# Sharing the expert outputs of a Perceiver block's mixture of experts among VectorE, ScalarE and GpSimd, and reordering the work around them

## The chip, the cores and the metric

The kernel runs on one core of a Trainium2 chip. The metric is the device time of one execution in microseconds; lower is better. The engines work side by side and are ordered by semaphores: TensorE (PE in the profile, its weight loads PEld), VectorE (DVE), ScalarE (ACT), GpSimd (POOL) and the sync engine (SP), which issues the DMAs. Each engine carries out its own instructions strictly in the order in which the program lists them.

## The reference

All numbers are float32. `x` holds 64 sequences of 32 rows of 256. Three sublayers follow one another, each added to `x`:

1. cross-attention to 257 context rows per sequence (4 heads, the 32 highest scores of each row kept), with a gain and shift from the attended context, a 32-step sequence convolution done by a real Fourier product, and a feed-forward part 256 -> 1024 -> 256;
2. self-attention over the 32 rows of each sequence (in the kernel called tile part c);
3. a mixture of 8 experts (tile part dd). For each row: `logits = x @ w_route.T` plus a product with normalized centroids; a softmax over the two highest logits gives `gate[8]`, zero elsewhere; then

```
out = x + sum_k gate[k] * (gelu(xn @ w1[k] + b1[k]) @ w2[k] + b2[k])      # k = 0..7, xn = layernorm(x)
```

## The kernel before

The 2048 rows are 16 tiles of 128 rows (4 sequences each). The kernel is a software pipeline that is written out by hand: 18 steps after a first one, and in step n four different tiles are at four stages: `a` (tile n: scores and the search for the 32 highest), `b` (tile n-1: attended context, gain and shift, Fourier convolution, first feed-forward product), `c` (tile n-2: end of the feed-forward part, self-attention) and `dd` (tile n-3: mixture of experts). Steps 3 to 15 hold all four; steps 16 to 18 run empty. There is one `step` function for each engine, and the order of the lines in it is the engine's order of work. `wait(engine, semaphore, value)` holds up the engine, and all that is listed behind it. The conditions are plain integers, since all steps are unrolled.

What the names around the change mean:

- `xl3` is the normalized input of the experts (L854 on VectorE, the first work of a step there; it is placed right behind L982 of the step before). PE transposes it at L1009 as the first thing after `down`, ahead of `scores(0)`. The two hidden products of the experts are `wide(0, D1, ...)` and `wide(1, D0, ...)`, 16 matmuls each (L1054), into the PSUM banks D1 and D0.
- `gelus(act2, 0, ...)` and `gelus(act2, 1, ...)` (L538) turn them into `act2` on ScalarE. In the step they stand behind the copy of `gateT` (L592, L593), which waits for PE's transpose of `gate` (L1135).
- `experts(range(...))` on PE multiplies `act2[k]` by `e_w2[k]` (L1071); experts 0, 1 go to D1, 2, 3 to D0, 4, 5 to D1, 6, 7 to D0. "Expert 8" is the product of `gateT` (8 rows) with `e_b2` (8 rows), the gated biases (L1069). A bank is overwritten after VectorE has read it.
- `gated(range(...))` on VectorE reads the banks: L842 and L844 start two sums `acc[0]` and `acc[1]`, L848 adds experts 2 to 7 to them in turn, L850 adds expert 8, and L982 adds the two sums into `out_sb`.
- `weights(t, q)` on GpSimd (L498, two instructions) makes `wsel[2q]`, `wsel[2q+1]` from VectorE's `rsum_row` (L833). PE's product `am` (L1101) of tile b needs all four. `norm(k, tile)` (L469 to L476) and `length(tile)` (L478 to L489) are chains of small GpSimd instructions that turn a variance into `rstd[k]` and `inorm`.
- `take(a, q)`, `top8`, `find8`, `take8` and `probs` on VectorE search for the 32 highest scores and make the attention weights; `probs(b, 1)` ends in L833.

GpSimd's order within a step is, shortened:

```
weights(b, 1); tm_tile (L503); xb_c (L507); norm(1, c); norm(2, c); norm(0, b); xt_b (L512); norm(3, c); length(c); weights(a, 0)
```

and VectorE's order at the end of one step and the start of the next:

```
top8(a,1,1); gated(6,8); top8(a,1,2); gated(8,9); L982   ||   L854 xl3; top8(b,1,3); probs(b,1) -> L833; L863; ...
```

Of the kernel before, what the change touches and what calls it, by code (L numbers as in the profile page):

```python
# [88 lines left out]
def build(nc, d, out):  # L89
    with ExitStack() as ctx:  # L90
# [6 lines left out]
        def sem(name):  # L97
            return ctx.enter_context(nc.semaphore(name))
# [27 lines left out]
        e_b2 = sb("e_b2", [NE, D])  # L126
# [18 lines left out]
        def over(buf, *shape):  # L145
# [7 lines left out]
            if len(shape) == 2:  # L153
# [55 lines left out]
        acc = [over("ang", D) for _ in range(2)]  # L209
        dots = sb("dots", [128, 2 * NE])  # L210
# [8 lines left out]
        gateT = sb("gateT", [NE, 128])  # L219
# [64 lines left out]
                 "xl3_v xT3_mm xT3_a lg_mm dots_a nbest_v ed_a gate_v gT_mm gT_a e1a_mm e1b_mm g2a_a g2b_a eo_mm acc_v fin_v").split()  # L284
# [3 lines left out]
        passed_v, passed_g = sem("passed_v"), sem("passed_g")  # L288
# [25 lines left out]
        def _(sp):  # L314
# [15 lines left out]
            for h in range(H):  # L330
# [9 lines left out]
            load(anyb[:, :], any_dram.rearrange("b o -> o b").broadcast_to([128, NB]), "ld_any")  # L340
            late_loads = [
# [9 lines left out]
                (e_b1[:, :], d["e_b1"], "ld_w"), (e_b2[:, :], d["e_b2"], "ld_w"),  # L351
# [44 lines left out]
        def _(pool):  # L396
# [26 lines left out]
            pool.wait_ge(s["fills"], 3)  # L423
            nc.gpsimd.memset(qk2[64:65, :, :, :], 1.0).then_inc(s["fills"], 1)
            nc.gpsimd.memset(zT2[64:65, :], 1.0).then_inc(s["fills"], 1)
            pool.wait_ge(s["fills"], 5)
# [64 lines left out]
            def step(a, b, c, dd):  # L491
                def weights(t, q):

                    wait_apart(pool, chains["tm"], t.count(1, 1), passed_g)
                    wait_apart(pool, s["rsum_v"], t.count(2, q + 1), passed_g)
                    wait_apart(pool, s["am_mm"], t.count(1, 0), passed_g)
                    for k in (2 * q, 2 * q + 1):
                        nc.gpsimd.tensor_scalar(wsel[:, k, :], sel[:, :], rsum_row[:, k:k + 1], tm_tile[:, k:k + 1], ALU.mult, ALU.mult).then_inc(s["wsel_g"], 1)  # L498
                if b:
                    weights(b, 1)  # L500
                if a:
                    wait_apart(pool, s["wsel_g"], a.count(4, 0), passed_g)
                    nc.gpsimd.tensor_copy(tm_tile[:, :], text_m[:, bass.ds(a.n * BT, BT)]).then_inc(chains["tm"], 1)  # L503
                if c:

                    wait_apart(pool, s["x1_v"], c.count(1, 0), passed_g)
                    nc.gpsimd.tensor_tensor(xb_c[:, :], x_all[:, c.n, :], bout[:, :], ALU.add).then_inc(s["xb_g"], 1)  # L507
                    norm(1, c)
                    norm(2, c)
                if b:  # L510
                    norm(0, b)
                    nc.gpsimd.tensor_tensor(xt_b[:, :], xt[:, :], b2[:, :], ALU.add).then_inc(s["xtb_g"], 1)  # L512
                if c:
                    norm(3, c)
                    length(c)
                if a:
                    weights(a, 0)

# [10 lines left out]
        def _(act):  # L529
# [31 lines left out]
            def step(a, b, c, dd, setup=None):  # L561
# [65 lines left out]
            act.wait_ge(s["fills"], 5)  # L627
# [29 lines left out]
        def _(dve):  # L657
# [128 lines left out]
            def step(a, b, c, dd):  # L786
# [48 lines left out]
                def gated(ks):  # L835

                    for k in ks:
                        bank = (D1, D0)[k // 2 % 2][:, k % 2 * D:k % 2 * D + D]
                        wait(dve, s["eo_mm"], dd.count(NE + 1, min(k // 2 * 2 + 2, NE + 1)))
                        if k == 0:  # L840
                            wait(dve, s["gate_v"], one(dd))
                            V.scalar_tensor_tensor(acc[0][:, :], bank, gate[:, 0:1], x2[dd.p][:, :], ALU.mult, ALU.add).then_inc(s["acc_v"], 1)  # L842
                        elif k == 1:
                            V.tensor_scalar(acc[1][:, :], bank, gate[:, 1:2], None, ALU.mult).then_inc(s["acc_v"], 1)  # L844
                        else:
                            wait(dve, s["acc_v"], dd.count(NE + 1, k - 1))
                            if k < NE:
                                V.scalar_tensor_tensor(acc[k % 2][:, :], bank, gate[:, k:k + 1], acc[k % 2][:, :], ALU.mult, ALU.add).then_inc(s["acc_v"], 1)  # L848
                            else:
                                V.tensor_tensor(acc[0][:, :], bank, acc[0][:, :], ALU.add).then_inc(s["acc_v"], 1)  # L850
# [105 lines left out]
                if dd:  # L956
                    gated(range(2, 4))
# [47 lines left out]
        def _(pe):  # L1005
# [26 lines left out]
            def step(a, b, c, dd, setup=None):  # L1032
# [25 lines left out]
                def experts(ks):  # L1058
                    for k in ks:
# [24 lines left out]
                if dd:  # L1084
                    wait(pe, s["xl3_v"], one(dd))
                    wait(pe, s["acc_v"], dd.count(NE + 1, 0))
# [16 lines left out]
                if dd:  # L1103
                    wide(0, D1, e_w1, xT3, None, range(2))
# [64 lines left out]
                if c:  # L1169
# [6 lines left out]
                    ins.then_inc(s["v_mm"], 1)  # L1176
                if c:
# [7 lines left out]
                if dd:  # L1185
                    experts(range(2, 4))
# [40 lines left out]
            pe.wait_ge(s["fills"], 5)  # L1227
# [132 lines left out]
```

## Time and profile before

| | |
|---|---|
| time, median of 3 runs | 695.81 us (691.54 to 697.91) |
| time of the profiled execution | 698.97 us |
| its span, first to last instruction | 697.1 us |
| mean granted TensorE clock in the span | 0.921 of full speed |
| busy time PE, PEld | 600.1 us (86%), 428.8 us (62%) |
| busy time DVE, ACT, POOL | 530.2 us (76%), 317.8 us (46%), 221.5 us (32%) |
| one full step | 34.38 us |

The profiled execution lies 1.9 us outside its span. The start-up and the first steps take up to 171 us, the 13 full steps run from there to about 616 us, and the rest is the emptying pipeline. Busy shares are averages over these three stretches. The length of a full step is the distance of equal instructions in the time line.

### The profile page before, as it was taken

How to read it: one execution, taken by the hardware profiler on the slowest of the kernel's cores; microseconds unless marked ns; L12 is line 12 of the kernel's file. 1: busy time of each engine (PE TensorE's matmuls, PEld its weight loads, DVE VectorE, ACT ScalarE, POOL GpSimd, SP SyncE). 2: the span in 40 equal slices, each digit the busy share in tenths (PEclk: the TensorE clock that was granted, in tenths of full speed). 3: DMA queues.
4: the chain of work that ended last, by engine and by line, in shares of the span. 5: the costliest groups of instructions: out<-in, count | busy, mean ns of one | idle time of the engine just before them, and what ended most of it. 6: DMA issues, size and time to landing. Idle time of an engine off the chain costs nothing.

```text
span 697.1 us, 12267 instructions
## 1 busy us (share of the span) xinstructions
PE 600.1 (86%) x4142; PEld 428.8 (62%) x4142; DVE 530.2 (76%) x1817; ACT 317.8 (46%) x793; POOL 221.5 (32%) x580
## 2 busy tenths in 40 slices
PE   0359367899999999999999999999999999988776
PEld 0135133647686868686868686868686858575655
DVE  5579956557797979788888888888888888875242
ACT  6432011414646464646454555555555555444422
POOL 2540301215151515152424242424242424252320
PEclk9968555869999999999999999999999999999876
DMA  5396032030302030302030203020302020000000
GB/s 163 81 263 174 9 139 72 0 97 1 97 9 98 9 98 9 97 9 97 9 97 9 98 9 97 9 97 9 98 12 94 17 89 9 1 9 1 8 9 8
DMA packets 18439, 40.33 MB, mean 58 GB/s; under 512 B 5093, under 2 KB 11190, under 8 KB 17864
## 3 DMA queue, kind: packets, MB, share of 16 engines
q1 hardware_dynamic: 18376, 39.55, 18.2%
q8 instruction: 33, 0.54, 0.3%
q14 instruction: 30, 0.25, 0.1%
HBM read 37.37 MB, written 2.16 MB: 57 GB/s over the span
## 4 chain that ended last, share of the span: by engine, by line
PE 72%; DVE 13%; ACT 9%; DMA 2%; issue 2%; POOL 1%; SPq 1%; ACTq 0%; DVEq 0%
PE D L1071 9%; PE D L1054 9%; PE BB L1054 8%; PE BB L1077 7%; PE S L1030 4%; ACT L538 3%; PE S L1046 3%; PE S L1047 3%; ACT ang L538 3%; PE BB L1131 2%; PE BB L1167 2%; PE PC L1173 2%; PE BB L1168 2%; PE BB L1132 2%; PE PC L1175 2%
## 5 line engine op out<-in xcount | busy, mean ns | idle before, releaser
L473 POOL TENSOR_SCALAR var_in<-mv 128x1 f32<-128x1 f32 x64 | 14.1, 221 | 321.6 <-DVE mv L938 164.5
L1071 PE MATMUL D<-expw,ang 128*128 128x256 f32 x256 | 74.3, 417 | 10.0 <-ACT ang L538 9.5
L821 DVE MATCH_REPLACE8 work<-top,work 128x257 f32<-128x257 f32 x192 | 77.4, 411 | 0.0
L1054 PE MATMUL D<-ang,e_w 128*128 128x128 f32 x512 | 72.0, 287 | 0.0
L815 DVE MAX8 top<-work 128x8 f32<-128x257 f32 x192 | 71.5, 414 | 0.0
L1054 PEld LDWEIGHTS D<-ang,e_w 128*128 128x128 f32 x512 | 64.0, 198 | 10.1 <-issue 10.1
L1054 PEld LDWEIGHTS BB<-ang,w 128*128 128x128 f32 x512 | 59.7, 192 | 7.7 <-issue 6.0
L1071 PEld LDWEIGHTS D<-expw,ang 128*128 128x128 f32 x256 | 46.3, 200 | 23.9 <-ACT ang L538 15.7
L1054 PE MATMUL BB<-ang,w 128*128 128x128 f32 x512 | 60.0, 275 | 0.0
L1077 PE MATMUL BB<-expw,ang 128*128 128x256 f32 x256 | 57.9, 379 | 0.0
L1046 PE MATMUL S<-ctx_t,qk 128*128 128x257 f32 x128 | 45.0, 436 | 11.7 <-DMA ctx_l<-in_ctx_l 5.0
L1077 PEld LDWEIGHTS BB<-expw,ang 128*128 128x128 f32 x256 | 47.4, 190 | 5.8
L498 POOL TENSOR_SCALAR wsel<-sel,rsum_row,tm_tile 128x32 f32<-128x32 f32 x64 | 25.8, 414 | 56.4 <-issue 31.4
L848 DVE SCALAR_TENSOR_TENSOR ang<-D,gate,ang 128x256 f32<-128x256 f32 x96 | 41.4, 474 | 2.0 <-PE D L1071 2.0
L1047 PE MATMUL S<-ctx_t,qk 65*128 65x257 f32 x128 | 42.9, 419 | 0.0
L1030 PE MATMUL S<-q_diag,wk_w 128*128 128x512 f32 x64 | 39.1, 704 | 3.6 <-ACT q_diag L551 3.6
L538 ACT ACTIVATE ang<-BB,b 128x128 f32<-128x128 f32 x128 | 36.6, 368 | 10.6 <-PE BB L1054 10.5
L538 ACT ACT_TABLE_LOAD x32 | 41.1, 1283 | 0.5
L569 ACT ACTIVATE expo<-S,nmax 128x257 f32<-128x257 f32 x64 | 27.0, 473 | 31.1 <-DVE work L801 30.8
L1046 PEld LDWEIGHTS S<-ctx_t,qk 128*128 128x128 f32 x128 | 23.3, 210 | 28.3 <-issue 26.9
L475 POOL TENSOR_TENSOR rstd<-var_in,mhalf 128x1 f32<-128x1 f32 x64 | 36.5, 571 | 5.3
L569 ACT ACT_TABLE_LOAD x28 | 35.9, 1283 | 0.5
(245 smaller groups left out, 1250.1 us busy)
## 6 DMA issues: line engine op xcount, KB each, us to landing
ctx_n<-in_ctx_n SPq DMA_DIRECT2D x16, 768.0 KB
ctx_t<-in_ctxT SPq DMA_DIRECT2D x16, 514.0 KB
ctx_t<-in_ctxT SPq DMA_DIRECT2D x16, 257.0 KB
x_all<-in_x SPq DMA_DIRECT2D x4, 512.0 KB, 5.5
out<-out_sb SPq DMA_DIRECT2D x16, 128.0 KB, 1.7
ctx_l<-in_ctx_l SPq DMA_DIRECT2D x64, 24.0 KB
w<-in_W SPq DMA_DIRECT2D x1, 1024.0 KB
e_w<-in_e_w SPq DMA_DIRECT2D x1, 1024.0 KB, 4.8
```

Source lines behind the costliest of these rows:

```text
L475: link(tt(rstd[k][:, 0:1], w, mhalf[:, 0:1], ALU.pow))
L538: ins = A(dst[:, k, :], bank[:, 128 * (k % 4):128 * (k % 4) + 128], ACT.Gelu, bias=bias[:, k:k + 1])
L569: A(expo[:, 2 * q + k, :], S[k][:, 0:G], ACT.Exp, bias=nmax[:, 2 * q + k:2 * q + k + 1], scale=SCALE).then_inc(s["exp_a"], 1)
L815: V.max(top[:, 2 * q + k, 8 * r8:8 * r8 + 8], work[:, 2 * q + k, :]).then_inc(chains["top"], 1)
L821: V.match_replace(work[:, 2 * q + k, :], top[:, 2 * q + k, 8 * r8:8 * r8 + 8], work[:, 2 * q + k, :], TAKEN).then_inc(chains["taken"], 1)
L848: V.scalar_tensor_tensor(acc[k % 2][:, :], bank, gate[:, k:k + 1], acc[k % 2][:, :], ALU.mult, ALU.add).then_inc(s["acc_v"], 1)
L1030: MM(S[half][:, :], wk_w[:, half, :], q_diag[:, :, :].rearrange("p h t -> p (h t)"), start=True, stop=True).then_inc(s["qk_mm"], 1)
L1046: MM(bank[:, 0:G], qk1[:, k, :, :].rearrange("p h t -> p (h t)"), ctx_t1[a.p][:, k, :], start=True, stop=False)
L1047: MM(bank[:, 0:G], qk2[:, k, :, :].rearrange("p h t -> p (h t)"), ctx_t2[a.p][:, k, :], start=False, stop=True).then_inc(s["sc_mm"], 1)
L1054: ins = MM(bank[:, 128 * m:128 * m + 128], w[:, k, at:at + 128], xs[:, 128 * k:128 * k + 128], start=k == 0, stop=k == 1)
L1071: MM(bank, act2[:, k, :], e_w2[:, k, :], start=True, stop=True).then_inc(s["eo_mm"], 1)
L1077: ins = MM(B1[:, 0:D], act1[:, k, :], w2[:, k, :], start=k == 0, stop=k == HID // 128 - 1)
```

## The change

1. PE: experts 2 and 3 are multiplied behind `v_mm` and ahead of the self-attention scores (`s_mm`), no longer behind them.
2. ScalarE: the first four gelus of the experts stand ahead of the copy of `gateT`.
3. PE: the bias product of "expert 8" uses 128 rows, zero-filled: `gateT` and `e_b2` grow from 8 to 128 partitions, with two more fills on GpSimd at the start.
4. VectorE keeps experts 0, 1, 4, 5 and 8, all summed in `acc[0]`. Experts 2, 3, 6 and 7 are scaled by `gate` and copied out of bank D0 by ScalarE into `e_out` (`outputs(0)`, `outputs(1)`). GpSimd sums the four into `acc[1]` with three additions behind `length(c)`; the first stands ahead of `weights(a, 0)` and two stand behind it. VectorE's last addition waits for them (`acc_g`).
5. Two semaphores that the unrolled kernel never uses are gone.

```
 # sync engine
+            sp.wait_ge(s["fills"], 5)                       # ahead of the late loads; e_b2 is loaded into e_b2[0:NE]
 # GpSimd, start
-            pool.wait_ge(s["fills"], 3)
+            nc.gpsimd.memset(gateT[:, :], 0.0).then_inc(s["fills"], 1)
+            nc.gpsimd.memset(e_b2[:, :], 0.0).then_inc(s["fills"], 1)
+            pool.wait_ge(s["fills"], 5)
 # GpSimd, step
                 if c:
                     norm(3, c)
                     length(c)
+                if dd:
+                    wait(pool, s["ge_a"], dd.count(2, 1))
+                    wait(pool, s["fin_v"], dd.count(1, 0))
+                    nc.gpsimd.tensor_tensor(acc[1][:, :], e_out[:, 0, :], e_out[:, 1, :], ALU.add).then_inc(s["acc_g"], 1)
                 if a:
                     weights(a, 0)
+                if dd:
+                    wait(pool, s["ge_a"], dd.count(2, 2))
+                    for k in range(2):
+                        wait(pool, s["acc_g"], dd.count(3, k + 1))
+                        nc.gpsimd.tensor_tensor(acc[1][:, :], acc[1][:, :], e_out[:, 2 + k, :], ALU.add).then_inc(s["acc_g"], 1)
 # ScalarE, step
+                def outputs(half):
+                    wait(act, s["eo_mm"], dd.count(NE + 1, 4 * half + 4))
+                    wait(act, s["gate_v"], one(dd))
+                    wait(act, s["acc_g"], dd.count(3, 2 * half - 2))
+                    for k in range(2):
+                        ins = A(e_out[:, 2 * half + k, :], D0[:, k * D:k * D + D], ACT.Copy, scale=gate[:, 4 * half + 2 + k:4 * half + 3 + k])
+                    ins.then_inc(s["ge_a"], 1)
...
                 if dd:
+                    gelus(act2, 0, D1, e_b1, "e1a_mm", "g2a_a", dd)
                     wait(act, s["gT_mm"], one(dd))
-                    copy(gateT[:, :], PA[0:NE, 0:128], "gT_a")
-                    gelus(act2, 0, D1, e_b1, "e1a_mm", "g2a_a", dd)
+                    copy(gateT[0:NE, :], PA[0:NE, 0:128], "gT_a")
                     gelus(act2, 1, D0, e_b1, "e1b_mm", "g2b_a", dd)
...
                 if following:
                     transposed(following)
+                if dd:
+                    outputs(0)
                 if c:
                     ... (r_c copy)
                 if following:
                     query(following)
+                if dd:
+                    outputs(1)
 # VectorE, step: gated() goes over (0, 1, 4, 5, NE), always acc[0], each waits for the one before
-                if dd:
-                    gated(range(2, 4))
...
-                if dd:
-                    gated(range(6, 8))
                 if a:
                     top8(a, 1, 2)
                 if dd:
                     gated(range(8, NE + 1))
-                    wait(dve, s["acc_v"], dd.count(NE + 1, NE + 1))
+                    wait(dve, s["acc_v"], dd.count(5, 5))
+                    wait(dve, s["acc_g"], dd.count(3, 3))
                     wait(dve, st_out[dd.p], dd.half(16, 0))
                     V.tensor_tensor(out_sb[dd.p][:, :], acc[0][:, :], acc[1][:, :], ALU.add).then_inc(s["fin_v"], 1)
 # PE, step
-                        elif k >= 4 and k % 2 == 0:
-                            wait(pe, s["acc_v"], dd.count(NE + 1, k - 2))
+                        elif k == 6:
+                            wait(pe, s["ge_a"], dd.count(2, 1))
+                        elif k in (4, 8):
+                            wait(pe, s["acc_v"], dd.count(5, k // 2))
...
                     ins.then_inc(s["v_mm"], 1)
+                if dd:
+                    experts(range(2, 4))
                 if c:
                     wait(pe, s["v_a"], one(c))
...
                     ins.then_inc(s["s_mm"], 1)
-                if dd:
-                    experts(range(2, 4))
```

## Rows read from the trace of the kernel before

**Rows 1.** Windows: busy time in four stretches, then granted clock, DMA share, GB/s

```profile
446.00:480.00 34.00, 33.05 (x251) 24.50 (x250) 28.86 (x107) 18.51 (x47) 12.11 (x34) 1.00 0.16 54
136.00:140.00 4.00, 2.20 (x21) 1.31 (x22) 2.40 (x8) 2.94 (x7) 0.46 (x2) 0.95 0.11 21
140.00:142.00 2.00, 2.00 (x3) 0.73 (x3) 0.37 (x2) 0.00 (x0) 1.25 (x4) 0.50 1.05 345
616.00:620.00 4.00, 3.11 (x25) 2.24 (x24) 3.37 (x15) 0.95 (x3) 1.89 (x6) 1.00 0.09 31
```

**Rows 2.** Time line of PE, one full step: start, duration, instruction, idle before

```profile
448.69 0.64 PE L1101 MATMUL PC<-prob,wsel 128*32 128x257 f32 x8
...
459.18 1.13 PE L1071 MATMUL D<-expw,ang 128*128 128x256 f32 x4 [0.20 <-ACT ang L538]
...
465.48 0.36 PE L1183 MATMUL PC<-ang 128*32 128x32 f32 x16 [0.75 <-ACT ang L533]
...
466.95 1.13 PE L1071 MATMUL D<-expw,ang 128*128 128x256 f32 x4
...
472.05 0.69 PE L1069 MATMUL D<-e_b,gateT 8*128 8x256 f32 x2
472.67 1.12 PE L1030 MATMUL S<-q_diag,wk_w 128*128 128x512 f32 x2
473.63 3.73 PE L1054 MATMUL BB<-ang,w 128*128 128x128 f32 x32
...
480.66 0.38 PE L1009 MATMUL D<-ident,ang 128*128 128x128 f32 x2
```

**Rows 3.** Time line of DVE, the same step and the start of the next

```profile
452.43 0.41 DVE L879 SCALAR_TENSOR_TENSOR z<-ctx_l,am,PC 128x192 f32<-128x192 f32 x1 [2.22 <-PE PC L1116]
...
466.42 0.48 DVE L844 TENSOR_SCALAR ang<-D,gate 128x256 f32<-128x256 f32 x1
...
472.30 0.18 DVE L774 BATCH_NORM_AGGREGATE mv<-bn 128x2 f32<-128x6 f32 x1
...
477.43 0.42 DVE L982 TENSOR_TENSOR out_sb<-ang 128x256 f32<-128x256 f32 x1
477.77 0.41 DVE L854 TENSOR_SCALAR ang<-ang,mv,rstd 128x256 f32<-128x256 f32 x1
...
480.35 0.17 DVE L833 RECIPROCAL rsum_row<-psum_row 128x2 f32<-128x2 f32 x1
480.86 0.42 DVE L863 TENSOR_TENSOR ang<-ang,BB 128x256 f32<-128x256 f32 x1 [0.34 <-PE BB L1077]
```

**Rows 4.** Time line of POOL, the same step and the start of the next

```profile
467.94 0.79 POOL L512 TENSOR_TENSOR ang<-ang,b 128x256 f32<-128x256 f32 x1
472.58 0.32 POOL L473 TENSOR_SCALAR var_in<-mv 128x1 f32<-128x1 f32 x1 [3.85 <-DVE mv L774]
...
477.71 0.90 POOL L498 TENSOR_SCALAR wsel<-sel,rsum_row,tm_tile 128x32 f32<-128x32 f32 x2
480.68 0.71 POOL L498 TENSOR_SCALAR wsel<-sel,rsum_row,tm_tile 128x32 f32<-128x32 f32 x2 [2.07 <-issue]
```

**Rows 5.** Time line of ACT, the same step: the copy of gateT

```profile
456.40 0.27 ACT L533 ACTIVATE gateT<-PC 8x128 f32<-8x128 f32 x1 [2.29 <-PE PC L1135]
```

**Rows 6.** Time line of DVE and POOL in step 2: one overlap

```profile
157.59 0.82 DVE L953 TENSOR_TENSOR pT_blk<-pT_c,block_mask 128x128 f32<-128x128 f32 x1
157.54 0.72 POOL L512 TENSOR_TENSOR ang<-ang,b 128x256 f32<-128x256 f32 x1
```

**Rows 7.** Time line of PE in the emptying steps 16 to 18

```profile
618.73 0.64 PE L1101 MATMUL PC<-prob,wsel 128*32 128x257 f32 x8 [0.41 <-POOL wsel L498]
...
658.36 2.08 PE L1071 MATMUL D<-expw,ang 128*128 128x256 f32 x4 [2.81 <-ACT ang L538]
...
686.43 6.72 PE L1071 MATMUL D<-expw,ang 128*128 128x256 f32 x16 [2.81 <-ACT ang L538]
```

**Rows 8.** Time line of DVE, start of step 18

```profile
674.89 0.41 DVE L854 TENSOR_SCALAR ang<-ang,mv,rstd 128x256 f32<-128x256 f32 x1 [0.62 <-POOL rstd L409]
```

More of the change, by code:

```diff
@@ L125, in build @@
         e_b1 = sb("e_b1", [128, NE])
-        e_b2 = sb("e_b2", [NE, D])
+        e_b2 = sb("e_b2", [128, D])
         dft_x = sb("dft_x", [128, NF])
@@ L209, in build @@
         acc = [over("ang", D) for _ in range(2)]
+        e_out = sb("e_out", [128, 4, D])
         dots = sb("dots", [128, 2 * NE])
@@ L218, in build @@
         gate = sb("gate", [128, NE])
-        gateT = sb("gateT", [NE, 128])
+        gateT = sb("gateT", [128, 128])
         out_sb = [sb(f"out_sb{i}", [128, D]) for i in range(2)]
@@ L283, in build @@
                  "xb_g x1_v st2_v rs2_g xl2_v xT2_mm xT2_a v_mm v_a s_mm nmaxc_v pc_a pt_v r_mm r_a o2_mm x2_v st3_v rs3_g inorm_g "
-                 "xl3_v xT3_mm xT3_a lg_mm dots_a nbest_v ed_a gate_v gT_mm gT_a e1a_mm e1b_mm g2a_a g2b_a eo_mm acc_v fin_v").split()
+                 "xl3_v xT3_mm xT3_a lg_mm dots_a nbest_v ed_a gate_v gT_mm gT_a e1a_mm e1b_mm g2a_a g2b_a eo_mm acc_v fin_v ge_a acc_g").split()
         s = {n: sem(n) for n in names}
         chains = {n: sem("self_" + n) for n in "tm g0 g1 g2 g3 len bn0 bn1 bn2 bn3 top taken u xhat xf logit best pg rsd yb rsc pn pT".split()}
-        passed_v, passed_g = sem("passed_v"), sem("passed_g")
+        passed_v, passed_g = None, None
         ld_x = [sem(f"ld_x{k}") for k in range(4)]
@@ L350, in _ @@
                 (wv_w[:, :, :], d["awvT"], "ld_w"), (wo_w[:, :, :], d["awoT"], "ld_w"), (route[:, :, 0:NE], d["routeT"], "ld_w"),
-                (e_b1[:, :], d["e_b1"], "ld_w"), (e_b2[:, :], d["e_b2"], "ld_w"),
+                (e_b1[:, :], d["e_b1"], "ld_w"), (e_b2[0:NE, :], d["e_b2"], "ld_w"),
             ]
@@ L422, in _ @@
             nc.gpsimd.memset(mhalf[:, :], -0.5).then_inc(s["fills"], 1)
-            pool.wait_ge(s["fills"], 3)
+            nc.gpsimd.memset(gateT[:, :], 0.0).then_inc(s["fills"], 1)
+            nc.gpsimd.memset(e_b2[:, :], 0.0).then_inc(s["fills"], 1)
+            pool.wait_ge(s["fills"], 5)
             nc.gpsimd.memset(qk2[64:65, :, :, :], 1.0).then_inc(s["fills"], 1)
             nc.gpsimd.memset(zT2[64:65, :], 1.0).then_inc(s["fills"], 1)
-            pool.wait_ge(s["fills"], 5)
+            pool.wait_ge(s["fills"], 7)
             are, aim, cre, cim = (s4[:, k, :] for k in range(4))
@@ L624, in step @@
                     gelus(act1, 1, B0, b1, "w1b_mm", "gb_a", b)
-            act.wait_ge(s["fills"], 5)
+            act.wait_ge(s["fills"], 7)
             act.wait_ge(s["ld_dt"], LD_DT)
@@ L835, in gated @@
                 def gated(ks):
-                    for k in ks:
-                        bank = (D1, D0)[k // 2 % 2][:, k % 2 * D:k % 2 * D + D]
+                    for i, k in enumerate((0, 1, 4, 5, NE)):
+                        if k not in ks:
+                            continue
+                        bank = D1[:, k % 2 * D:k % 2 * D + D]
                         wait(dve, s["eo_mm"], dd.count(NE + 1, min(k // 2 * 2 + 2, NE + 1)))
@@ L842, in gated @@
                             V.scalar_tensor_tensor(acc[0][:, :], bank, gate[:, 0:1], x2[dd.p][:, :], ALU.mult, ALU.add).then_inc(s["acc_v"], 1)
-                        elif k == 1:
-                            V.tensor_scalar(acc[1][:, :], bank, gate[:, 1:2], None, ALU.mult).then_inc(s["acc_v"], 1)
                         else:
-                            wait(dve, s["acc_v"], dd.count(NE + 1, k - 1))
+                            wait(dve, s["acc_v"], dd.count(5, i))
                             if k < NE:
-                                V.scalar_tensor_tensor(acc[k % 2][:, :], bank, gate[:, k:k + 1], acc[k % 2][:, :], ALU.mult, ALU.add).then_inc(s["acc_v"], 1)
+                                V.scalar_tensor_tensor(acc[0][:, :], bank, gate[:, k:k + 1], acc[0][:, :], ALU.mult, ALU.add).then_inc(s["acc_v"], 1)
                             else:
@@ L1085, in step @@
                     wait(pe, s["xl3_v"], one(dd))
-                    wait(pe, s["acc_v"], dd.count(NE + 1, 0))
+                    wait(pe, s["ge_a"], dd.count(2, 0))
                     transposes(D0, xl3, "xT3_mm")
@@ L1103, in step @@
                 if dd:
+                    wait(pe, s["acc_v"], dd.count(5, 0))
                     wide(0, D1, e_w1, xT3, None, range(2))
@@ L1226, in _ @@
             pe.wait_ge(s["ld_cent"], LD_CENT)
-            pe.wait_ge(s["fills"], 5)
+            pe.wait_ge(s["fills"], 7)
             def film_products():
```

## The prediction

> **What bounds the kernel now.** I read the windows first, then the time lines of the four engines over one full step, then the chain of waits. In a full step PE is busy 33.05 of 34 us at full clock [rows 1]; the step repeats every 34.38 us (PE's L1009 at 446.28 and at 480.66 [rows 2]). The chain of waits runs over PE for nearly the whole step. PE idles at two places: 0.36 us ahead of experts 0 and 1, which wait for gelus that stand behind the copy of `gateT` (the time line shows 0.20 of it in brackets), and 0.75 us ahead of the self-attention scores [rows 2, 5]. DVE is the second bound: it works without a break from 459.18 to 480.52, and PE's experts 4 and 5 start at 466.95, 0.05 us behind the end of L844 at 466.90 [rows 2, 3]. DVE's only long idle time is 2.22 us ahead of L879 [rows 3]. POOL has little work, but it lies in a queue: from `st3_v` (DVE's L774, ending at 472.48) it needs until 477.62 for `norm(3)` and `length`, then `weights(a, 0)` follows at 477.71 and `weights(b, 1)` at 480.68, 0.16 us after the `rsum_row` that it needs [rows 3, 4].
>
> **Parts 1 to 3, PE.** The gelus no longer wait for the gate, so PE's first wait of 0.36 us goes, and experts 2 and 3 fill the 0.75 us ahead of the scores. But both savings end at DVE: its run from 459.18 to L844 waits for nothing that these edits move, and experts 4 and 5 cannot start before it. PE waits there instead. L844 becomes an addition onto `acc[0]` and so must wait for L842: independent ones start 0.39 apart, a dependent one starts its own 0.48 plus about 0.04 later, so it ends 0.13 later, and experts 4 and 5 start at about 467.08 [rows 2, 3]. Behind that, the padded bias product gains: L1069 starts at 472.05 and the next matmul at 472.67, 0.62 us for two matmuls of 256 columns and 8 rows. Full matmuls are faster: L1054 does 32 of 128 columns in 3.57 us (3.73, of which some 0.16 is the drawn-out end of the last), 0.111 each, so 256 columns take 0.22 and two take 0.44. The two of 512 columns behind the small product take 0.96 (472.67 to 473.63) instead of 0.89, and the transposes ahead of it some 0.09 more than elsewhere [rows 2]. An 8-row product thus costs its neighbours time as well: 0.18 + 0.07 + 0.09 = 0.34, all of it taken as gained. Bounds: 0 (if the fill of 128 rows is no faster) to 0.34; I take the upper one, since all other 128-row products go at that rate. Net for PE: 0.34 - 0.13 = 0.2 us a step. On ScalarE nothing of it costs: it had 2.29 us idle there [rows 5]. Start-up: two fills and a wait that they meet long before; nothing.
>
> **Part 4, DVE.** Four of ten additions go, 4 x 0.43 = 1.7 us of DVE work, two of them ahead of `x2`. `x2` then waits for PE's product `o2_mm` instead of DVE's queue; by the time line that product was done 0.32 us before `x2` started and now comes 0.13 later, so `st3_v` comes about 0.19 us earlier than 472.48 (bounds 0 and 0.4). Without the queue on POOL the parts together would give 0.2 us a step.
>
> **Part 4, the queue on POOL.** The three additions stand behind `norm(3)` and `length`, and VectorE's last addition waits for all three. Behind that wait on DVE stand `xl3`, `top8(b, 1, 3)` and `probs(b, 1)` with `rsum_row`; for `xl3` waits PE ahead of the next step's scores, for `rsum_row` waits POOL's `weights(b, 1)`, and for that PE's `am`. An addition of 128x256 on POOL took 0.79 us here and 0.72 in step 2 [rows 4, 6]; I take 0.75 and 0.06 to 0.10 for each wait. From 477.62: first addition 0.09 + 0.75, `weights(a, 0)` 0.07 + 0.90, second 0.07 + 0.75, third 0.10 + 0.75: 3.48 us, done at 481.10 instead of DVE's turn at 477.43.
>
> **The new loop.** From PE's `am` to `am` of the next step:
> - `am` at 448.69 to `st3_v` at 472.48 less 0.19: 23.60 [rows 2, 3]
> - to the end of `length`: 5.14 [rows 3, 4]
> - the additions and `weights(a, 0)`: 3.48
> - `acc_g` to the start of L982: 0.05; L982 to the end of L833 (477.43 to 480.52): 3.09 [rows 3]
> - to the end of `weights(b, 1)` at 481.39: 0.88 [rows 4]; to PE: 0.06
>
> Sum 36.30 us against 34.38: **+1.92 us a step**. PE, ready for `xl3` at 480.4, waits 1.3 us for it, and then 0.8 us more for `wsel` at `am`. What gives slack again behind `am`: DVE is 3.2 us late at L863 but waits at L879 for PE, 2.22 us before; `am` itself is 1.9 late, so it still arrives 1.2 us early. `norm(1)` on POOL ends about 1 us before DVE needs it. The DVE idle ahead of L982 becomes about 4.6 us.
>
> The trace has no scaled copy of 128x256 by ScalarE; the like unscaled ones (L533, L614) take 0.38, and scaling may add nothing or as much again. Four a step: 0 to +1.5 us of ScalarE, which has 18.51 busy of 34 [rows 1]; experts 6 and 7 need the first pair by 469.3 and it is ready by 467.6, so it costs 0. I take 0.
>
> **Twelve steps.** The first `am` that is late is step 4's, the last full one step 15's: 12 x 1.92 = 23.0 us.
>
> **The emptying pipeline.** Step 15 to 16 had `am` at 618.73, 32.53 us behind step 15's (448.69 + 4 x 34.38 = 586.20), since no scores stood in between [rows 2, 7]. The loop over POOL hardly shrinks (36.0): +3.5. In step 17 the experts wait 2.81 us for the gelus, and behind that wait PE runs at half clock: 2.08 us for the four matmuls that take 1.13 at full [rows 2, 7]. The gelus now come before the gate, PE's gap is near 0.5 us, and the clock should hold: about -4.7 at `x2`. From there `xl3` of step 18, which waited only for `rstd` [rows 8], now waits for `length` (2.9), three additions (2.45) and L982 (0.4): +5.8. In step 18 the experts start 2.9 us earlier than 686.43 [rows 7], but the scaled copies and the additions hang behind the last products (+1.4): -1.5. Sum 3.5 - 4.7 + 5.8 - 1.5 = +3.1.
>
> **Sum.** 23.0 + 3.1 = +26 on a span of 697.1: 723 us, with 1.9 outside 725. The median of the runs is 3.2 below the profiled execution: **722 us**.
>
> **Where the Trainium skill comes in.** The trace shows the same elementwise addition at 0.42 us on DVE and 0.72 to 0.79 on POOL, and L953, normally 0.29, drawn out to 0.82 while POOL's L512 ran [rows 3, 4, 6]. The Trainium skill, GPSIMD Engine Reference, section Engine selection, speaks against this change: an elementwise addition on a tile belongs on VectorE, GpSimd being about twice as slow for two inputs. Its section Specifications adds that GpSimd shares its SBUF interfaces with VectorE, with contention for VectorE instructions with two SBUF inputs. If each addition took twice DVE's 0.42 us, an estimate from that page, the three would last 0.27 us longer than I take, and the time would be 725. The measured durations decide here, and the sum goes by them.
>
> **Rivals.**
> - *The additions find room*: if DVE's stall were absorbed somewhere, 0.2 x 13 = 3 us would be gained in the full steps and up to 6 in the emptying ones: 687 to 693. Against it: the program order on both queues; for it only the 4.6 us of DVE idle, which nothing listed may use. 5%. If half of the stall were absorbed (POOL's steps shorter than I took), about 700 to 708: 7%.
> - *Contention*: each of POOL's additions holds up a DVE instruction for up to 0.75 us. Two of the three fall into DVE's new idle time, the first too; what remains is L512 against `xhat` (467.9, 0.03 us apart in my time line): +0.4 a step at most, 727. Inside the forecast.
> - *The clock falls.* PE now idles 2.1 us within 4.6 at each boundary. The granted clock stayed at 1.00 from 616 to 620 with 0.9 idle of 4, but was at half from 140 on, after 1.8 idle of the 4 us before, in gaps of no more than 0.6 us in the time line [rows 1]. If each boundary brought some 5 us at 1.2 GHz, PE would lose 2.5 us a step, 12 x 2.5 = 30: 752. [...] 12%.
>
> **Chances and range.** Forecast 76% (contention included), clock 12%, half absorbed 7%, fully absorbed 5%. Bounds of the forecast: POOL's additions at 0.72 and waits at nothing, the drain at +0: +1.5 a step, 714; additions at 0.85, the `xhat` delay and a drain without the clock's gain (+3): 735. Range 711 to 738. Runs of this kernel tell about 1% from no change. Faster by over 1%: 0.04; within 1%: 0.05; slower by over 1%: 0.91.
>
> **What would show it.** Right: a full step of 36.0 to 36.6 us; DVE idle of over 4 us ahead of the last addition, released by POOL; PE's L1009 on `xl3` idle for over 1 us, released by DVE; `am` released by POOL; the next matmul 0.44 us behind the bias product; experts 2 and 3 ahead of the scores and no 0.75 us gap; clock 1.00 in full steps. Wrong: `weights` or `norm(3)` much shorter than here, a step near 34.2, or a clock below 1.00 in full steps.

## The result and the profile after

| | before | after |
|---|---|---|
| median of the runs, us | 696.14 (691.54 to 697.91, 4 runs) | 718.55 (715.81 to 719.97, 4 runs) |
| ratio, 95% interval | | 1.033 (1.027 to 1.039) |
| span of the profiled execution, us | 697.1 | 717.9 |
| full step, `am` to `am`, us | 34.38 | 35.87 |
| start up to `am` of step 3, us | 173.7 | 174.3 |
| 12 full steps, `am` of step 3 to `am` of step 15, us | 412.6 | 430.5 |
| from `am` of step 15 to the end, us | 110.9 | 113.2 |

The change makes the kernel 22 us slower. Of the 20.8 us by which the span grew, 12 x 1.49 = 17.9 are full steps, 2.3 the emptying pipeline and 0.6 the start. Line numbers of the changed kernel are some 22 higher than before.

The page of the changed kernel, busy time by engine: DVE is less busy than before, and the kernel is slower.

```profile
span 717.9 us, 12334 instructions
PE 593.6 (83%) x4142; PEld 429.4 (60%) x4142; DVE 504.1 (70%) x1753; ACT 340.3 (47%) x857; POOL 252.3 (35%) x630
```

The windows of one full step and of two stretches of step 16 (columns as in [rows 1]):

```profile
486.00:522.00 36.00, 33.27 (x255) 25.08 (x254) 27.64 (x106) 19.94 (x52) 14.19 (x38) 1.00 0.17 51
636.00:640.00 4.00, 1.09 (x10) 0.79 (x12) 3.90 (x17) 0.57 (x2) 0.89 (x3) 0.82 0.10 33
640.00:644.00 4.00, 4.00 (x22) 3.19 (x23) 0.71 (x2) 0.85 (x3) 2.11 (x6) 0.50 0.00 0
```

Taken from one `am` to the next, PE is busy for 33.15 of 35.87 us, before for 33.43 of 34.38, both at full clock: its work is the same and the step has 1.5 us more. The time line of PE shows where they lie. It answers to [rows 2]:

```profile
461.26 0.64 PE L1126 MATMUL PC<-prob,wsel 128*32 128x257 f32 x8 [0.77 <-POOL wsel L502]
...
478.56 0.41 PE L1032 MATMUL PC<-ident,xln 128*128 128x128 f32 x2 [0.58 <-DVE xln L804]
479.61 1.13 PE L1096 MATMUL D<-expw,ang 128*128 128x256 f32 x4 [0.64 <-DVE ang L874]
...
484.61 0.60 PE L1094 MATMUL D<-e_b,gateT 128*128 128x256 f32 x2
485.05 1.02 PE L1053 MATMUL S<-q_diag,wk_w 128*128 128x512 f32 x2
485.90 3.73 PE L1077 MATMUL BB<-ang,w 128*128 128x128 f32 x32
493.82 0.44 PE L1032 MATMUL D<-ident,ang 128*128 128x128 f32 x2 [0.73 <-DVE ang L880]
```

The two waits of before (0.20 in brackets and 0.75) are gone. Four others stand in their place: 0.58 ahead of the transposes of `xln` and 0.64 ahead of experts 4 and 5, then 0.73 at `xl3` and 0.77 at `am`, the two that start and end with POOL. Here is POOL's time line over the boundary (against [rows 4]):

```profile
489.70 0.23 POOL L493 TENSOR_SCALAR inorm<-var_in 128x1 f32<-128x1 f32 x1
490.02 0.73 POOL L524 TENSOR_TENSOR ang<-e_out 128x256 f32<-128x256 f32 x1
490.73 0.71 POOL L502 TENSOR_SCALAR wsel<-sel,rsum_row,tm_tile 128x32 f32<-128x32 f32 x2
491.40 1.53 POOL L531 TENSOR_TENSOR ang<-ang,e_out 128x256 f32<-128x256 f32 x2
```

And DVE's time line at the same place (against [rows 3]):

```profile
484.65 0.18 DVE L800 BATCH_NORM_AGGREGATE mv<-bn 128x2 f32<-128x6 f32 x1
...
493.02 0.42 DVE L1005 TENSOR_TENSOR out_sb<-ang 128x256 f32<-128x256 f32 x1 [4.05 <-issue]
493.36 0.41 DVE L880 TENSOR_SCALAR ang<-ang,mv,rstd 128x256 f32<-128x256 f32 x1
```

The reader is to see one chain through three engines: `st3_v` at 484.83 (L800), the end of `length` at 489.93 (L493), then addition, `weights(a, 0)` and two additions without a gap until 492.93, then DVE's L1005 at 493.02 after 4.05 us of idle time. L880 (`xl3`), for which PE waits at 493.82, stands behind it. The bracket says "issue" because the queue shows no single releaser for the wait. The view of all waits names POOL where the wait is longest:

```profile
DVE out_sb L1005 <- issue: 44.6, 11, 4.1
DVE out_sb L1005 <- POOL ang L531: 23.8, 5, 7.1
```

### The profile page after: what moved, and what is told of

Its sections match the earlier page's. It is cut to its first block and busy times, and to the rows that moved or that the text cites. A ratio compares the mean times of both kernels' runs of the same rounds, so it can differ in the third digit from the quotient of the medians.

```text
span 717.9 us, 12334 instructions
## 1 busy us (share of the span) xinstructions
PE 593.6 (83%) x4142; PEld 429.4 (60%) x4142; DVE 504.1 (70%) x1753; ACT 340.3 (47%) x857; POOL 252.3 (35%) x630
## 5 line engine op out<-in xcount | busy, mean ns | idle before, releaser
L477 POOL TENSOR_SCALAR var_in<-mv 128x1 f32<-128x1 f32 x64 | 14.0, 219 | 295.8 <-DVE mv L964 163.8
L1096 PE MATMUL D<-expw,ang 128*128 128x256 f32 x256 | 67.8, 388 | 12.4 <-DVE ang L874 11.8
L1077 PE MATMUL D<-ang,e_w 128*128 128x128 f32 x512 | 75.4, 297 | 0.0
L1077 PEld LDWEIGHTS D<-ang,e_w 128*128 128x128 f32 x512 | 67.3, 207 | 10.5 <-issue 10.5
L1005 DVE TENSOR_TENSOR out_sb<-ang 128x256 f32<-128x256 f32 x16 | 7.3, 453 | 68.4 <-issue 44.6
L502 POOL TENSOR_SCALAR wsel<-sel,rsum_row,tm_tile 128x32 f32<-128x32 f32 x64 | 23.3, 376 | 71.0 <-issue 48.0
L547 ACT ACTIVATE ang<-D 128x256 f32<-128x256 f32 x16 | 6.1, 383 | 63.8 <-PE D L1032 63.8
```

The costliest lines, as they stand in the source:

```text
L1077: ins = MM(bank[:, 128 * m:128 * m + 128], w[:, k, at:at + 128], xs[:, 128 * k:128 * k + 128], start=k == 0, stop=k == 1)
L1096: MM(bank, act2[:, k, :], e_w2[:, k, :], start=True, stop=True).then_inc(s["eo_mm"], 1)
```

## The experiments

Two theories stood against each other. *Queue position*: the loss comes from where the three additions stand, between `length` and the last addition, so that a wait chain PE, DVE, POOL, DVE, PE sets the step. *Work and sharing*: the additions cost by themselves, by their length on GpSimd and by slowing VectorE's work beside them, so the loss comes wherever they run. Times are medians beside runs of the kernel before on the same chip. The full step of each is the median of the twelve distances between ScalarE's copies of `dots` (steps 3 to 15) in its trace; most of them agree within 0.02 us, and nothing that differs at the start or the end enters it.

### e1: the same additions, earlier in POOL's queue

```
+                if dd: (first addition)                # was behind length(c)
                 if c:
                     norm(3, c)
+                if dd: (second and third addition)      # were behind weights(a, 0)
+                if c:
                     length(c)
                 if a:
                     weights(a, 0)
```

> The changed kernel with GpSimd's three additions moved ahead in its queue: the first ahead of norm(3), the other two between norm(3) and length; nothing else. Queue theory (the cost is that VectorE's last addition waits for additions that stand behind norm(3), length and weights): the additions end at about 488.7 on the changed kernel's time line, when VectorE's own last product sum ends at 488.97, so the wait goes; a full step falls from 35.86 to 34.1 to 34.2 us, the time to 686 to 694 us. Work theory (the copies and additions cost by themselves, by contention for memory or a fuller ScalarE): the step stays above 35 us, the time above 708.

Measured: 683.74 us (before 694.66), ratio 0.982 (0.975 to 0.988); full step 34.07. The same instructions on the same engines gain 1.80 us a step over the changed kernel, and are faster than before. POOL's and DVE's time lines of this kernel:

```profile
461.15 0.73 POOL L521 TENSOR_TENSOR ang<-e_out 128x256 f32<-128x256 f32 x1
...
466.87 1.54 POOL L528 TENSOR_TENSOR ang<-ang,e_out 128x256 f32<-128x256 f32 x2
```

```profile
468.80 0.43 DVE L1006 TENSOR_TENSOR out_sb<-ang 128x256 f32<-128x256 f32 x1
```

The additions last as long as in the changed kernel, and the last addition on DVE has no idle time ahead of it. So it is the place that costs, not the work.

### e2: additions left late, the wait for them moved

`final` (the waits for `acc_v`, `acc_g` and the store, and the last addition) goes from the end of step n on DVE to step n+1, behind `xl3`, the logits and `best`. The additions stay as they are in the changed kernel.

```
                     V.max(best[:, :], logit[:, :]).then_inc(chains["best"], 1)
+                if dd and dd.n:
+                    final(Tile(dd.base, dd.c - 1))
```

> The changed kernel with GpSimd's order kept, but VectorE's last addition of a tile moved into the next step, ahead of L905 (z), where VectorE waits for PE anyway. Queue theory: the additions still end late, but xl3, the search and rsum_row no longer stand behind them; step 34.1 to 34.4 us, time 686 to 696 us. If instead the late wsel (GpSimd's own queue, weights behind the additions) were the cost, PE would still wait at am: step 35 us or more.

Measured: 681.06 us, ratio 0.981 (0.976 to 0.986); full step 34.07. The same step as e1 with the other end of the chain cut. What cost was what stood behind DVE's wait, not the additions ahead of it.

### e3: one addition more in the queue

```
+                    nc.gpsimd.tensor_tensor(junk[:, :], e_out[:, 0, :], e_out[:, 1, :], ALU.add).then_inc(s["junk_g"], 1)
```

It stands ahead of the first addition, and nothing reads its result.

> The changed kernel with one more addition of 128x256 on GpSimd ahead of the three, into a tile that nobody reads. Queue theory: each microsecond of GpSimd work between length and acc_g lengthens the step by itself: +0.75 us a step, step 36.6, in 12 full steps +9, with the emptying steps +11: 728 to 731 us. Slack theory (VectorE's wait ends somewhere that has room): within 2 us of the changed kernel.

Measured: 725.98 us, ratio 1.046 (1.042 to 1.051); full step 36.58, which is 0.71 more than the changed kernel's. POOL's time line:

```profile
492.15 0.73 POOL L526 TENSOR_TENSOR junk<-e_out 128x256 f32<-128x256 f32 x1
492.84 0.72 POOL L527 TENSOR_TENSOR ang<-e_out 128x256 f32<-128x256 f32 x1
```

The starts are 0.69 apart; the step grows by the whole length of the addition. So the chain through POOL is the one that sets the step, with no slack beside it.

### e4, e5, e6: parts 1 to 3 without part 4

e4 is the changed kernel with part 4 undone: eight scaled additions on DVE and none on POOL. e5 is the kernel before with the padded bias product alone, e6 the kernel before with the two orders (parts 1 and 2) alone:

```
 # e6, ScalarE
+                    gelus(act2, 0, D1, e_b1, "e1a_mm", "g2a_a", dd)
                     wait(act, s["gT_mm"], one(dd))
                     copy(gateT[:, :], PA[0:NE, 0:128], "gT_a")
-                    gelus(act2, 0, D1, e_b1, "e1a_mm", "g2a_a", dd)
 # e6, PE
                     ins.then_inc(s["v_mm"], 1)
+                if dd:
+                    experts(range(2, 4))
...
                     ins.then_inc(s["s_mm"], 1)
-                if dd:
-                    experts(range(2, 4))
```

> The kernel before with the first three parts alone: experts 2, 3 ahead of the scores, first gelus ahead of the gate copy, padded bias product. Sums stay on VectorE in two chains. By the prediction's terms: bias product -0.34 us a step, the other two nothing in full steps (VectorE bounds that stretch), so step 34.0 to 34.1 us, -4; emptying steps -6 (experts no longer wait for the gate, clock held): 684 to 690 us. If PE's two waits had been the bound: -1.1 us a step, 675.

> The kernel before with the padded bias product alone. The prediction gave it 0.34 us a step: step 34.04 us. The order changes alone gave 0.11 and all three together 0.50, so if the parts add up it is 0.39: step 33.99. If the filled rows were worth nothing: 34.38.

> The kernel before with parts 1 and 2 alone (experts 2, 3 ahead of the scores, first gelus ahead of the gate copy); bias product of 8 rows, sums as before. If VectorE bounds the stretch from the Fourier product to experts 4 and 5, PE's 1.11 us of waits only move: full step 34.2 to 34.4 us, with PE idle ahead of the transposes of xln and of experts 4 and 5 instead. If PE's waits were the bound: 33.3 us. With part 3 alone the parts should add up to the step of 33.88 us that all three gave: 0.50 in all, of which the prediction gave 0.34 to the bias product.

Measured: e4 676.93 us, ratio 0.976 (0.972 to 0.979), full step 33.88. One run each gave 691.59 for e5 (step 33.99) and 681.32 for e6 (step 34.27). In full steps the bias product is worth 0.39 us and the orders 0.11, and the sum of 0.50 is what e4 has. The emptying pipeline, from the copy of `dots` of step 15 to the end, is the reverse: 98.9 us in e4 and 99.7 in e6 against 110.8 before. e5's 110.2 shows no more than the steps give. So the gain there is from the orders. What is left of PE's waits in e4, from its time line:

```profile
457.59 0.41 PE L1012 MATMUL PC<-ident,xln 128*128 128x128 f32 x2 [0.58 <-DVE xln L781]
458.45 1.13 PE L1074 MATMUL D<-expw,ang 128*128 128x256 f32 x4 [0.45 <-DVE ang L847]
```

And all of DVE's idle times in one step of e4 that the time line shows:

```profile
440.05 0.43 DVE L797 MAX8 top<-S 128x8 f32<-128x257 f32 x1 [0.44 <-PE S L1050]
444.04 0.41 DVE L882 SCALAR_TENSOR_TENSOR z<-ctx_l,am,PC 128x192 f32<-128x192 f32 x1 [2.22 <-PE PC L1119]
447.90 0.42 DVE L909 TENSOR_TENSOR ang<-xhat,BB 128x256 f32<-128x256 f32 x1 [0.93 <-PE BB L1135]
449.59 0.69 DVE L919 TENSOR_TENSOR had<-BB,kern_f 96x512 f32<-96x512 f32 x1 [0.48 <-PE PC L1151]
```

From L919 at 449.59 to the next step DVE has no gap: PE's waits of 0.36 and 0.75 us have come back as waits of 0.58 and 0.45 us for DVE, as the prediction has it, and only 0.1 us is gained.

### e7: only the sum of experts 0 and 1 chained

e4 with expert 1 added onto `acc[0]` by DVE (as in the changed kernel) instead of starting `acc[1]`; `acc[1]` starts with expert 3.

```
+                        elif k == 3:
+                            V.tensor_scalar(acc[1][:, :], bank, gate[:, 3:4], None, ALU.mult)
+                            if k == 1:
+                                V.scalar_tensor_tensor(acc[0][:, :], bank, gate[:, 1:2], acc[0][:, :], ALU.mult, ALU.add)
```

> The kernel with parts 1 to 3, but expert 1 is added onto acc[0] behind expert 0 (and expert 3 starts acc[1]), as the changed kernel's VectorE does it. By the prediction each step gets 0.13 us longer: 34.0 against 33.88. The kernels with part 4 and no queue stall run at 34.07; if the chain is all of it, this one runs at 34.07 too; if the ScalarE copies or GpSimd additions cost something in the step, it stays below.

Measured: 683.46 us in one run, full step 34.08: 0.20 more than e4, and equal to e1 and e2. DVE's time line of e7, then of e4:

```profile
462.95 0.47 DVE L845 SCALAR_TENSOR_TENSOR ang<-D,gate,ang 128x256 f32<-128x256 f32 x1
463.52 0.48 DVE L851 SCALAR_TENSOR_TENSOR ang<-D,gate,ang 128x256 f32<-128x256 f32 x1
```

```profile
457.53 0.47 DVE L845 SCALAR_TENSOR_TENSOR ang<-D,gate,ang 128x256 f32<-128x256 f32 x1
457.92 0.47 DVE L847 TENSOR_SCALAR ang<-D,gate 128x256 f32<-128x256 f32 x1
```

The dependent addition starts 0.57 us behind its predecessor (0.58 in e1), the independent one 0.39. Two things follow. The dependence costs 0.2 us a step. And e1, with 1.7 us less work for DVE and four scaled copies more for ScalarE, is at the same 34.07: once the queue is right, taking these four additions off DVE changes the step by no more than 0.01, since what they free lies behind the stretch that PE waits for.

### e8 and e9: the room on DVE used for the search

To use what part 4 frees, the rounds `top8(a, 0, 2)` and `(a, 0, 3)` of the search were moved behind the norms into the second half of DVE's step: in e8 on top of e4, in e9 on top of e1.

```
                     top8(a, 0, 1)
-                    top8(a, 0, 2)
...
-                    find8(a, 0, 3)
-                    take8(a, 0, 3)
...
+                    top8(a, 0, 2)
+                    top8(a, 0, 3)
                     probs(a, 0)
```

> Parts 1 to 3 on the kernel before, and on VectorE top8(a, 0, 2) and top8(a, 0, 3) moved behind the statistics of x2, ahead of probs(a, 0): 1.45 us of search leaves the stretch that ends at PE's experts 4 and 5. Theory that this stretch bounds PE: the waits of PE there (0.58 + 0.45 us) go, step 32.8 to 33.1 us, time 662 to 670 us. Theory that VectorE's total work bounds (it has the same work as before): the step stays above 33.6, with new waits of PE at xl3 or am.

> The same move of the search on the changed kernel with GpSimd's additions early. VectorE has 1.7 us less work a step here, ScalarE and GpSimd more. If the stretch bounds PE: step 32.8 to 33.1 us as well, so that the sharing of the sums gives nothing. If VectorE's total work bounds once the search is moved, this one is faster than parts 1 to 3 with the search moved, by up to 0.5 us a step.

Measured: e8 697.51 us, ratio 1.003 (0.999 to 1.007), step 35.20; e9 705.19 us, ratio 1.012 (1.003 to 1.020), step 35.54. Moving both rounds (2.9 us) overfills the second half. In e8, PE's time line has the waits at the boundary that the changed kernel has, now with no addition on POOL:

```profile
486.14 0.44 PE L1010 MATMUL D<-ident,ang 128*128 128x128 f32 x2 [0.33 <-DVE ang L857]
489.44 0.64 PE L1102 MATMUL PC<-prob,wsel 128*32 128x257 f32 x8 [0.77 <-POOL wsel L501]
```

e9 has less work on DVE than e8 and is 0.34 us a step slower. It also has the dependent addition of e7, and its additions on POOL run beside DVE's work. DVE's, POOL's and PE's time lines of e9:

```profile
470.79 0.81 DVE L975 TENSOR_SCALAR pn_c<-p_c,rsum_c 128x32 f32<-128x32 f32 x1
...
471.88 0.51 DVE L979 TENSOR_TENSOR pT_blk<-pT_c,block_mask 128x128 f32<-128x128 f32 x1
...
475.51 0.42 DVE L989 TENSOR_TENSOR ang<-ang,PC 128x256 f32<-128x256 f32 x1 [1.49 <-PE PC L1234]
...
479.73 0.95 DVE L856 SCALAR_TENSOR_TENSOR prob<-work,expo 128x257 f32<-128x257 f32 x1
```

```profile
470.84 0.73 POOL L516 TENSOR_TENSOR ang<-ang,b 128x256 f32<-128x256 f32 x1
471.52 0.72 POOL L521 TENSOR_TENSOR ang<-e_out 128x256 f32<-128x256 f32 x1
...
478.63 1.77 POOL L528 TENSOR_TENSOR ang<-ang,e_out 128x256 f32<-128x256 f32 x2
```

```profile
452.70 0.64 PE L1125 MATMUL PC<-prob,wsel 128*32 128x257 f32 x8 [0.77 <-POOL wsel L502]
...
470.74 1.13 PE L1095 MATMUL D<-expw,ang 128*128 128x256 f32 x4 [0.96 <-DVE ang L875]
472.45 0.65 PE L1225 MATMUL PC<-ang,pT_blk 128*32 128x64 f32 x32 [0.58 <-DVE pT_blk L979]
```

In e8 `pn_c` takes 0.24 us and `prob` 0.42; here they are drawn out by 0.57 and 0.53 us while a POOL addition runs, and POOL's pair takes 1.77 instead of 1.53. (`pT_blk` is drawn out in both: 0.51 here, 0.60 in e8, 0.29 in the kernel before.) `pn_c` lies ahead of the product that DVE awaits at L989, `prob` ahead of `rsum_row` and so of `am`. The time lines tell how they add up. From `am` to experts 4 and 5 e9 takes 18.04 us and e8 17.85: 0.19, the size of the dependent addition in e7. From there to `x2` (L989) e9 takes another 0.40 more, and PE waits 0.58 for `pT_blk`, which it does not in e8. From `x2` to the next `am` DVE has no gap in either, and e9, with fewer additions there, is 0.24 shorter although `prob`'s 0.53 lie in it. So both drawn-out instructions lie on the path, and 0.19 of the difference has nothing to do with POOL. No run has the additions moved away from just these two instructions.

One full step of e9 took 37.17 us: PE had waited 0.95 and 0.58 us between 539 and 543.5, as in every step, and this time the granted clock of the window from 543 to 547 was 0.59.

### e10 and e11: a better mixture

e10 is e1 with e2's late `final`, and expert 0's addition moved ahead of `nmax_c`, so that expert 1's no longer waits for it. e11 is e10 with one round of the search moved instead of two: `top8(a, 0, 2)` goes to the place of round 3, and round 3 goes in front of `probs(a, 0)`.

```
 # e10                                       # e11, besides
+                if dd:                      -                    top8(a, 0, 2)
+                    gated(range(0, 1))      -                    find8(a, 0, 3); take8(a, 0, 3)
                 if c: (nmax_c)              +                    top8(a, 0, 2)
-                    gated(range(0, 2))      ...
+                    gated(range(1, 2))      +                    top8(a, 0, 3)
```

> The changed kernel with GpSimd's additions early, the final addition late (both as in the earlier runs), and VectorE's sum of expert 0 ahead of the maximum of the self-attention scores, so that expert 1 need not stand directly behind it. The chain between experts 0 and 1 cost 0.19 us a step; this hides it: step 33.85 to 33.95 us, against 34.07 with either move alone. If the swap only delays the maximum and what hangs on it: 34.1 or more.

> The same with one round of the search (1.45 us) moved out of the stretch ahead of PE's experts 4 and 5 into the place of the next round, and that round behind the statistics of x2. VectorE has about 1.4 us idle ahead of L863's addition in this version. If PE's waits in the stretch (about 1 us) bound: step 33.0 to 33.4 us, 655 to 670 us. If VectorE's work in the second half and GpSimd's additions beside it bound: 33.8 us or more, with PE waiting at am.

Measured: e10 682.52 us, ratio 0.983 (0.978 to 0.989), step 33.98; e11 678.15 us, ratio 0.975 (0.970 to 0.980), step 33.72. Taking the dependence apart gives back 0.10 us of the 0.20, the search 0.26 more. e11's step lies between the two that were expected, and PE does not wait at `am`. PE in e11 still waits twice in the middle:

```profile
458.57 1.13 PE L1105 MATMUL D<-expw,ang 128*128 128x256 f32 x4 [0.37 <-DVE ang L882]
460.17 0.65 PE L1235 MATMUL PC<-ang,pT_blk 128*32 128x64 f32 x32 [0.47 <-DVE pT_blk L990]
```

e11 has the shortest step of all, e4 the better time by 1.2 us; the two can't be told apart, and both beat the kernel before by 2.5%.

### e12: part 4 alone

The kernel before with part 4 (and, as e5 has it, the padded buffers and their fills, but not the padded product): `gateT[0:NE]` and `e_b2[0:NE]` are multiplied.

> The changed kernel with parts 1 to 3 undone: late gelus, experts 2 and 3 behind the scores, bias product of 8 rows; the sums stay shared. The loop over GpSimd runs from am through x2 and its statistics, the additions and the next wsel. If it alone sets the step, only what lies between am and x2 counts: the two edits that only fill waits (0.11 us as measured) come back, and PE's later bias product does not; step 35.9 to 36.2 us. If the savings of parts 1 to 3 added to the loop in full: 36.36.

Measured: 727.43 us in one run, full step 35.98. Part 4 costs 1.60 us a step on the kernel before and 1.99 on e4 (33.88 to 35.87). Parts 1 to 3 bring 0.50 us without it and 0.11 with it. That follows from the chain: they can shorten it only between `am` and `st3_v`, and that stretch has 23.67 us in e12 and 23.57 in the changed kernel. The rest of their gain is PE's, and PE waits for the chain.

## Why the prediction was right, and where its sizes were off

**The mechanism.** It was right: the additions stand in POOL's queue between `length` and DVE's last addition, and `xl3` and `rsum_row` stand behind DVE's wait for them. e1 and e2 cut the chain at either end and both gain 1.80 us a step; e3 lengthens it by one addition and the step grows by 0.71. The DVE idle of over 4 us, the two waits of PE at the boundary, the bias product with the next matmul 0.44 us behind it and the full clock in full steps all showed as the prediction has them. One sign did not come: PE waits 0.73 us for `xl3`, not over 1. The full step, 35.87, lies just below the 36.0 to 36.6 that were given.

**The sum of the loop**, term by term:

| term | predicted | measured |
|---|---|---|
| `am` to `st3_v` | 23.60 | 23.57 |
| to the end of `length` | 5.14 | 5.10 |
| additions and `weights(a, 0)` | 3.48 | 3.00 |
| to L1005, and on to `rsum_v` | 0.05 + 3.09 | 0.09 + 3.09 |
| `weights(b, 1)`, then PE | 0.88 + 0.06 | 0.87 + 0.15 |
| sum | 36.30 | 35.87 |

One term was mis-sized: the work on POOL, by 0.48 us a step. The prediction took 0.75 for an addition and 0.06 to 0.10 for every wait, and 0.90 for `weights` [rows 4]. Measured, back to back: addition, `weights` and the pair follow each other at 0.71, 0.67 and 1.53. Waits that are already met add nothing that shows, and `weights` took 0.71 here. Of its two rows of before, 0.90 at 477.71 and 0.71 at 480.68 [rows 4], the second was the better basis: at the first, DVE's L982 and L854 ran beside it [rows 3], and in the changed kernel DVE is idle there. That fits what e9 shows of the two engines, but no run isolates it. This term makes 12 x 0.48 = 5.8 us; the others take back 0.05 a step, so the full steps gave 17.9 us where 23.0 was forecast. That is the main part of the difference between 725, forecast for the profiled execution, and the 719.97 that it took. The median shows 3.5 of it, since it lies only 1.4 below that execution and not 3.2 as before.

**The terms that the loop hid.** The bias product gained 0.39 us where 0.34 was taken (e5), the dependent addition cost 0.20 where 0.13 was taken (e7), and the orders brought 0.11 in full steps where nothing was taken (e6). ScalarE's scaled copies took 0.83 to 0.84 us a pair and raised its busy time from 18.51 to 19.91 us a step, within the 0 to 1.5 that were given; the step did not show them: e1 with them is at 34.07, e7 without them at 34.08.

**The emptying pipeline.** The sum was near (+3.1, measured 113.2 - 110.9 = +2.3) and its make-up was not. `am` of step 16 came 35.24 us behind that of step 15, +2.7 instead of +3.5. In step 16 the clock then fell, which the prediction has only as a rival for full steps. PE's time line of the changed kernel:

```profile
636.66 0.44 PE L1032 MATMUL D<-ident,ang 128*128 128x128 f32 x2 [1.89 <-DVE ang L880]
637.57 0.62 PE L1119 MATMUL D<-route,ang 128*128 128x16 f32 x4 [0.47 <-ACT ang L547]
639.97 1.08 PE L1126 MATMUL PC<-prob,wsel 128*32 128x257 f32 x8 [1.77 <-POOL wsel L502]
```

PE had 1.09 us of work in 4 from 636, the granted clock was 0.50 in the next 4, and `am` took 1.08 us instead of 0.64. From step 16's `dots` to step 17's it took 37.1 us instead of 32.4, and from there to the end 42.6 instead of 46.4. The gain from the orders came, as foreseen in kind, but is larger: e4, without part 4, has 98.9 us from `dots` of step 15 on, where the kernel before has 110.8 and the changed one 113.9. Some 0.8 of the last belong to the full steps (the `am` of step 15 still waits behind its `dots`). Part 4 thus costs 14 us in the emptying pipeline, not the 7.8 that the terms +3.5, +5.8 and -1.5 hold, and the orders, with the prediction's 4.7, gain 11 to 12 without it (e4, e6). By this count two errors of some 6 to 7 us met and cancelled. The count hangs on the kernel in the middle, though. e12, part 4 alone, has 120.1 us from `am` of step 15 to the end, against 110.9 before and 113.2 in the changed kernel: there part 4 costs 9.2 and the other parts bring 6.9, near the 7.8 and 4.7 of the prediction. The two overlap in the emptying steps by some 5 us, which the prediction's sum does not have. That its total was near is thus in part luck; each kernel has one trace here.

**The rivals.** *The additions find room* fell, but its condition is what e1 and e2 make true. *Contention* was not seen in the changed kernel's step; e9 shows that it is real where POOL's additions meet short DVE work on the path. *The clock falls* did not happen at the boundaries of the changed kernel's full steps, with waits of 0.73 and 0.77 us, and did in its emptying steps, in step 16 behind waits of 1.89, 0.47 and 1.77. That the rival was a real one shows in e9, which lost 1.6 us in one full step of twelve that way.

**Where the change's cost lies**, with e4 as the middle: parts 1 to 3 take 12 x 0.50 = 6.0 us from the full steps and 11.9 from the emptying ones; part 4 adds 12 x 1.99 = 23.9 and some 14. With e12 as the middle part 4 adds 12 x 1.60 = 19.2 and 9.2, and parts 1 to 3 then take 1.3 and 6.9.

## What to carry to other kernels

Work given to an idle engine lands at a place in its queue, and so does the wait for it: before moving it, list what stands behind both, and put the work where the engine would idle (here ahead of `norm(3)` and `length`), and the wait behind whatever others need. A queue theory has a cheap proof, one dummy instruction more in it: where the queue alone sets the step, the step grows by the whole length, as in e3, and with slack it would grow by less. Taking work off an engine pays only in the stretch that someone waits for.

## What the runs showed of the hardware that was not expected

- **Small products cost their neighbours.** Two matmuls of 256 columns with 8 rows, padded to 128 rows of zeros, made the full step 0.39 us shorter (e5): twice the 0.18 that they themselves lasted longer. The Trainium skill, TensorEngine Tiling (Array Packing), section Key Properties, says that changing the tiling mode drains TensorE. The gain fits that, but no run here shows whether these products change the mode, nor separates a drain from a slower fill.
- **GpSimd and VectorE draw each other out.** In e9 `pn_c` took 0.81 us where e8 has 0.24, one of the two `prob` 0.95 where e8 has 0.42, and POOL's pair of additions 1.77 instead of 1.53. Not every overlap does it: the other `prob`, at 479.39, ran beside the same pair and took 0.42. The Trainium skill, GPSIMD Engine Reference, section Specifications, names contention for VectorE instructions in a 2-port perf mode or with two SBUF inputs. `prob` and `pT_blk` have two; `pn_c`, drawn out the most, has one tensor and a scalar of each partition, and no run shows the mode in which it ran.
- **A dependent addition in place** on DVE starts 0.57 to 0.58 us behind its predecessor, an independent one 0.39 (e1, e7 and e4); on PE's path that was 0.20 us a step (e7).
- **The start-up differs by up to 10 us between traces of kernels that are nearly alike there**: 163.8 us to `dots` of step 3 in e2, 168.6 in e1, 173.2 in e7, 174.4 in the changed kernel. The page of the changed kernel has its granted clock as the first row below, that of e2 as the second. e2 holds more of its clock after the first stretch, and no edit explains it. Each kernel has one trace, so it can be the execution as well as the kernel: e2's traced execution, 677.30 us, was the fastest of four that reach to 683.99. The cause stays open.

```profile
PEclk9998555869999999999999999999999999989987
```

```profile
PEclk9999588989999999999999999999999999999998
```

The times of one kernel's executions differ by about 1% (691.54 to 697.91 us before), while the full steps within a trace repeat to a few hundredths of a microsecond, save one step of e9 (37.17) and one of e12 (36.28 at full clock, not explained). So small changes are better read from the step than from the whole time.
